# Feed-forward, context MLP and routing as one pipeline, and attention transposes one slot later

## The reference

```python
x = x + _L0_xattn_ref(_layernorm(x), ctx, ctx, mask0, bias, ...)   # attention, 16 heads of 16
x = x + _L0_ffn_ref(_layernorm(x), W_r, W_k, W_v, mu_r, mu_k)
x = x + _L1_xattn_ref(_layernorm(x), ctx, ctx)                     # gelu(x ctx^T) ctx
x = x + _L1_ffn_ref(_layernorm(x), w_router, w1, w2, w3)           # 8 experts, best 2
x = x + _L2_xattn_ref(_layernorm(x), ctx, ctx, W, b, mask2)        # attention, causal
x = x + _L2_ffn_ref(_layernorm(x), gate_w, shared..., r_...)       # shared + best 1 of 8
x = x + _L3_xattn_ref(_layernorm(x), ctx, ctx, Wq, Wk, Wv, Wo)     # attention, score 0 masked
x = x + _L3_ffn_ref(_layernorm(x), weight_int8, weight_scale, bias)
# inside _L0_ffn_ref, with x_prev the tokens shifted by one
r = sigmoid((mu_r * x + (1 - mu_r) * x_prev) @ W_r.T)
k = (mu_k * x + (1 - mu_k) * x_prev) @ W_k.T
out = r * (square(relu(k)) @ W_v.T)
```

## Time and profile before

| | us |
|---|---|
| median of 3 runs | 1191.1 (1186.71 to 1192.58) |
| the profiled execution, its own time | 1189.59 |
| span of its trace | 1187.9 |
| TensorE busy | 915.3 (77%) |
| VectorE busy | 567.6 (48%) |
| ScalarE busy | 424.1 (36%) |
| GpSimd busy | 404.0 (34%) |

### The profile page before, as it was taken

One profiled execution on the slowest core, in us unless ns is written; L12 is line 12 of the kernel. 1 busy time (PEld: TensorE's weight loads), 2 busy tenths in 40 slices (PEclk: granted clock), 3 DMA queues, 4 the chain that ended last, 5 costly groups with the idle time before them and its releaser, 6 DMA issues. The chain is left out here.

```text
span 1187.9 us, 18637 instructions
## 1 busy us (share of the span) xinstructions
PE 915.3 (77%) x5578; PEld 605.2 (51%) x5579; DVE 567.6 (48%) x1207; ACT 424.1 (36%) x820; POOL 404.0 (34%) x741
## 2 busy tenths in 40 slices
PE   6688757867229999963777867997999978877773
PEld 5455536643216777742444523664666655545541
DVE  4778845644431222225899713221121225777764
ACT  4355532312003333312666522221222213555644
POOL 5656634422470000016776411110000022666550
PEclk9899978968559999985899887998999996887885
DMA  5690001000121111124710030001111110000002
GB/s 169 241 327 1 1 4 45 0 10 0 49 102 49 62 62 62 62 68 159 293 32 19 1 107 22 23 26 58 36 44 44 40 46 14 15 14 14 1 1 71
DMA packets 60183, 71.25 MB, mean 60 GB/s; under 512 B 8172, under 2 KB 51924, under 8 KB 60116
## 3 DMA queue, kind: packets, MB, share of 16 engines
q1 hardware_dynamic: 55507, 57.81, 14.6%
q0 software_dynamic: 4608, 12.59, 3.2%
HBM read 45.73 MB, written 24.64 MB: 59 GB/s over the span
## 5 line engine op out<-in xcount | busy, mean ns | idle before, releaser
L1566 PE MATMUL PS<-WE,tmp 128*128 x496 | 185.8, 518 | 0.0
L1219 DVE TENSOR_TENSOR tmp<-PS,tmp 128x352 f32<-128x352 f32 (+1 forms) x78 | 47.4, 608 | 261.6 <-ACT tmp L858 261.6
L543 POOL TENSOR_TENSOR tmp<-tmp,small 128x616 f32<-128x616 f32 x96 | 116.7, 1216 | 102.1 <-DVE small L995 101.5
L1566 PEld LDWEIGHTS PS<-WE,tmp 128*128 128x128 f32 x496 | 91.5, 194 | 60.4 <-issue 36.1
L858 ACT ACTIVATE tmp<-PS 128x352 f32<-128x352 f32 (+1 forms) x78 | 41.4, 531 | 218.8 <-PE PS L1566 218.8
L771 ACT ACTIVATE tmp<-PS 128x768 f32<-128x768 f32 x96 | 77.9, 811 | 115.5 <-PE PS L1390 114.9
L1388 PE MATMUL PS<-ident,tmp 128*128 128x128 f32 x384 | 69.2, 309 | 45.1 <-POOL rsx L530 26.1
L1586 PE MATMUL PS<-WE,tmp 128*128 (+1 forms) x418 | 101.0, 380 | 2.1 <-DVE tmp L1231 2.1
L1301 PE MATMUL PS<-ident,XN 128*128 128x128 f32 x240 | 48.4, 337 | 68.2 <-ACT XN L707 54.0
L508 POOL DMA_INDIRECT WE<-ys,slot_u x32 | 32.5, 1015 | 182.4 <-DMA ys<-tmp 172.7
L644 POOL DMA_INDIRECT xs<-tmp,slot_u x48 | 46.6, 971 | 121.7 <-DVE tmp L1206 112.0
(11 more groups left out here) (210 smaller groups left out, 1620.8 us busy)
## 6 DMA issues: line engine op xcount, KB each, us to landing
tmp<-xs SPq DMA_DIRECT2D x62, 128.0 KB, 2.0
ys<-tmp SPq DMA_DIRECT2D x62, 128.0 KB, 1.7
xs<-WE SPq DMA_DIRECT2D x4, 1536.0 KB, 9.5
WE<-in_L_w SPq DMA_DIRECT2D x16, 352.0 KB, 6.9
WE<-in_L_rgT SPq DMA_DIRECT2D x8, 512.0 KB, 10.0
WE<-in_L_ruT SPq DMA_DIRECT2D x8, 512.0 KB, 10.2
WE<-in_L_rdT SPq DMA_DIRECT2D x8, 512.0 KB, 10.3
X<-in_x SPq DMA_DIRECT2D x8, 256.0 KB, 6.8
```

The costliest lines, as they stand in the source:

```text
L543: pool.tensor_tensor(sc, sc, spread(mx[:, q], SK), ALU.add).then_inc(shifted, 1)
L1219: dve.tensor_tensor(HH[:, q, 0:F], PS[:, 2 * q + 1, 0:F], SL[:, q, 0:F], ALU.mult).then_inc(hh_ready, 1)
L1566: last = pe.matmul(PS[:, 2 * q + k, 0:F], XS[:, q, c], w, start=c == 0, stop=c == G - 1)
```

## The change

1. f0, m1 and r1 with its scatter become one stage, f, of 12 slots (`F_SLOTS`). In slot s the engines do: keys and gates of batch s; values, sum, layernorm and transposes of the feed-forward of batch s-1; the MLP of batch s-2; the transposes, logits and best two experts (`two_experts`) of batch s-3; ranks, slots (`two_slots`) and four indirect DMAs of batch s-4.
2. So that a token's slot can be known before all tokens are routed, each expert has a region of 2176 rows in `xs1_regions` (8 regions and one tile: 137 tiles, all zeroed, 12 DMAs of up to 1.5 MB instead of 4). `expert_tables` afterwards works out which tiles are used, and SyncE reads each tile's first row from SBUF (`value_load`). The number of tiles in e1 is still 39.
3. The shifted tokens are multiplied by ScalarE instead of GpSimd (`previous`). The sigmoid is 0.5 * (1 + tanh(x / 2)), which leaves one activation table for the stage; compiled, the stage has one table load less than f0, m1 and r1. Normalising moves from VectorE to ScalarE.
4. `W_k`, `W_v`, the router's weights and the context are loaded during a0; only `W_r` and a2's output weights are loaded after it.
5. `value_blocks` for a2 run at the end of f, in eight PSUM banks without waiting for one another.
6. In all three attentions the transposes of unit s-3 follow the scores of unit s, the values are those of s-4, and on VectorE bias and maximum come ahead of the sums. The slots of the output projection, the residual and what follows are one later; those of the gathers and of the way in are two earlier.

The diff, cut to its core:

```diff
-        def out_proj_slot(b):
-            return UNITS * b + 7
+            return UNITS * b + 8
...
         def gather_slot(b, t, k, K):
-            return UNITS * b - 11 + t * 2 + k * (2 // K)
+            return UNITS * b - 13 + t * 2 + k * (2 // K)
...
         def in_transpose_slot(b):
-            return UNITS * b - 4
+            return UNITS * b - 6
...
+            xs1, xs2 = BUFS["e1"][0], BUFS["e2"][0]
+            for s in range(F_SLOTS):
+                if 0 <= s - 4 < B:
+                    scatter_rows(s - 4, 0)
+                if 0 <= s - 1 < B:
+                    deviations_and_shifts(F_NORM["ffn", s - 1], s - 1)
+                if 0 <= s - 2 < B:
+                    deviations_and_shifts(F_NORM["mlp", s - 2], s - 2)
+                if 0 <= s - 4 < B:
+                    scatter_rows(s - 4, 1)
...
+                    if 3 <= s < NU + 3:
+                        u = s - 3
+                        act.wait_ge(pt_psum, u0 + u + 1)
+                        after(act, ot_ready, (u0 + u) // 2 - 1 if u >= 4 else 0)
+                        act.activation(PT[:, u % 4], PT_PSUM, ACT.Copy).then_inc(pt_ready, 1)
...
+            for s in range(F_SLOTS):
+                if s < B:
+                    mixes(s)
+                if 0 <= s - 1 < B:
+                    add_ffn(s - 1)
+                    row_stats(F_NORM["ffn", s - 1], s - 1)
+                if 0 <= s - 4 < B:
+                    two_slots(s - 4)
+                if 0 <= s - 2 < B:
+                    add_mlp(s - 2)
+                    row_stats(F_NORM["mlp", s - 2], s - 2)
+                if 0 <= s - 3 < B:
+                    two_experts(s - 3)
+            expert_tables()
+            end_stage(dve, "f")
...
                     if 0 <= s < NU:
                         scores(s)
-                    if s == 3:
+                    if 3 <= s < NU + 3:
+                        transposes(s - 3)
+                    if s == 4:
                         pe.wait_ge(blocks_ready, 4 * (layer + 1))
-                    if 3 <= s < NU + 3:
-                        values(s - 3)
+                    if 4 <= s < NU + 4:
+                        values(s - 4)
...
-                    if 2 <= s < NU + 2:
-                        transposes(s - 2)
...
+            for i, banks in enumerate(FREE_BANKS):
+                if i == 3:
+                    pe.wait_ge(rank_taken, B)
+                value_blocks(1, i, banks)
+            end_stage(pe, "f")
```

More of the change, by code:

```diff
@@ L718, in attention @@
                 u0, q0 = NU * layer, 0 if stage == "a0" else B
[L719 removed]
+                order = ORDER[stage]
                 def queries(b):
@@ L1120, in running_sums, with mixes @@
                 return ping
-            def route(stage, first):
-                to = dict(r1="e1", r2="e2")[stage]
-                K, n_slots = TOPK[to], SLOTS[to]
+            def mixes(b):
+                dve.wait_ge(prev_ready, b + 1)
+                for dst, prev, k, used, ready in ((xkT, tB, 3, k_psum, k_mixed), (xrT, tA, 2, r_psum, r_mixed)):
+                    after(dve, used, b)
+                    for g in range(G):
+                        last = dve.scalar_tensor_tensor(out=dst[:, g], in0=XT[:, b, g, 1:S + 1], scalar=vecs[:, k, g:g + 1],
+                                                        in1=prev[:, g], op0=ALU.mult, op1=ALU.add)
+                    last.then_inc(ready, 1)
@@ new lines, in two_experts @@
+            def two_experts(b):
+                tiles = slice(b * T, (b + 1) * T)
+                dve.wait_ge(logits_psum, b + 1)
+                dve.tensor_copy(LG[:, tiles], PS[:, 4, 0:T * E].rearrange("p (t e) -> p t e", t=T)).then_inc(logits_copied, 1)
+                dve.drain()
+                first_of(LG[:, tiles], 0, tiles)
+                dve.scalar_tensor_tensor(out=count[:, 1, tiles], in0=hot[:, 0, tiles], scalar=NEG, in1=LG[:, tiles],
+                                         op0=ALU.mult, op1=ALU.add)
+                dve.drain()
+                first_of(count[:, 1, tiles], 1, tiles)
+                dve.tensor_tensor(taken[:, tiles], hot[:, 0, tiles], hot[:, 1, tiles], ALU.add).then_inc(pair_taken, 1)
@@ L1252, in _ @@
             dve.drain()
-            for i in range(B // 2):
-                value_blocks(1, i)
             experts("e1")
@@ new lines, in ffn_values, with mlp_hidden @@
+            def ffn_values(b):
+                pe.wait_ge(ksq_ready, b + 1)
+                after(pe, r_used, b)
+                two_tiles(6, ksq, W[:, 2]).then_inc(v_sum, 1)
+            def mlp_hidden(b):
+                pe.wait_ge(xt_ready, F_NORM["ffn", b] + 1)
+                after(pe, g_ready, b)
+                for c in range(G):
+                    last = pe.matmul(PS[0:SK, 2, 0:S], ctxT[:, c, b * SK:(b + 1) * SK], XT[:, b, c, 1:S + 1],
+                                     start=c == 0, stop=c == G - 1)
+                last.then_inc(g_psum, 1)
@@ new lines, in mlp_out, with logits @@
+            def mlp_out(b):
+                pe.wait_ge(g_ready, b + 1)
+                after(pe, c_taken, b)
+                for t in range(T):
+                    last = pe.matmul(PS[:, 3, t * D:(t + 1) * D], gel[:, t * P:(t + 1) * P], V[:, b], start=True, stop=True)
+                last.then_inc(c_psum, 1)
+            def logits(b):
+                pe.wait_ge(xt_ready, F_NORM["mlp", b] + 1)
+                after(pe, logits_copied, b)
+                for t in range(T):
+                    for c in range(G):
+                        last = pe.matmul(PS[:, 4, t * E:(t + 1) * E], XT[:, b, c, 1 + t * P:1 + (t + 1) * P], WR[:, c],
+                                         start=c == 0, stop=c == G - 1)
+                last.then_inc(logits_psum, 1)
@@ new lines, in _ @@
+            pe.wait_ge(w_loaded, 16 * 7)
+            pe.wait_ge(ctx_loaded, 16 * 2)
+            pe.wait_ge(tri_ready, 1)
+            for s in range(F_SLOTS):
+                if 0 <= s - 1 < B:
+                    ffn_values(s - 1)
+                if 0 <= s - 3 < B:
+                    transpose_rows(F_NORM["mlp", s - 3], ND[(s - 3) % 3])
+                if 0 <= s - 2 < B:
+                    mlp_hidden(s - 2)
+                if 0 <= s - 4 < B:
+                    ranks(s - 4)
+                if s < B:
+                    ffn_keys(s)
+                if 0 <= s - 2 < B:
+                    mlp_out(s - 2)
+                if 0 <= s - 3 < B:
+                    logits(s - 3)
+                if s < B:
+                    ffn_gates(s)
+                if 0 <= s - 1 < B:
+                    transpose_rows(F_NORM["ffn", s - 1])
@@ L1594, in experts @@
                 end_stage(pe, stage)
-            pe.wait_ge(w_loaded, 16 * 7)
-            route("r1", 0)
-            for i in range(B // 2):
-                value_blocks(1, i)
             pe.wait_ge(blocks_ready, 8)
```

547 lines of the change are left out of this document (289 added, 258 removed).

## The result

The changed kernel takes 1237.37 us (median of 4, 1230.33 to 1239.78) against 1191.32 us: the ratio is 1.038, with a 95% interval of 1.033 to 1.044. The prediction was 1136 us, with a range of 1110 to 1168, so the sign was wrong.

A forecast was written before the change was run, and what follows sets the result against it. No engine was taken as full from a0's end to e1's start; VectorE was taken as fullest in the attentions. 1189.6 - 32.6 - 9 - 2 - 11 = 1135, 1136 us with run-to-median difference; range 1110 to 1168.

The forecast's parts named there:

- part 2: a0: the wait of 1.48 us at the residual goes, period 13.0 us a batch; -9 us, range -10 to 0.
- parts 3 and 4: a2: nothing steady, -2 us, range -6 to +4; a3: ScalarE's copy no longer waits, -11 us, range -19 to +3.
- The attentions keep their periods: Rival, chance 0.15: in the attentions the same wait may only change its place; starts and tails alone left, 1167 us.
- part 4: a3: rsx transposes follow the next scores, ScalarE's copy stops waiting, 17.7 to 18.0 us a batch, start +6.8; -11 us.
- the term of +3.2: a2's start: first scores may come behind batch 1's transposes, 3.2 us after the first bias of the kernel before.
- the ramp's waits: a2's ramp: the bias waits, 6.9 us in all, were to go in part.
- Part 1: Stage f: full slots of 13.5 us, TensorE fullest at 12.7; e1 starts at 322.7, not 355.3; -32.6 us, range -40 to -8.
- the loop rival: Rival, chance 0.20: f's slot is one serial loop with handovers costing as in f0; 16.5 us a slot, +25, 1160 us.
- the clock rival: Rival, chance 0.04: TensorE's clock stays low in f; all slots at 1.2 GHz give +75, 1210 us.
- the rival had it at 1 us a tile: Rival, chance 0.03: SyncE's register loads do not hide in e1; 39 tiles give +39, 1175 us.
- The lead of 8.8 us: e1: SyncE reads the row address and fetches two tiles, 8.8 us, ahead, so e1 was left at zero.

The follow-up runs named there:

- f_only: The changed kernel with all three attentions written as before (part 6 undone), the stage f kept: 1161.58 us, ratio 0.977.
- The best version: Stage f, register load hoisted, two value blocks in f's last slots, a3 with later transposes, VectorE's old order and earlier blocks, a0 and a2 as before: 1136.43 us.

## Why the prediction was wrong

**The step that failed** is in part 2, and parts 3 and 4 lean on it: "what is late next is VectorE itself: 12.03 busy and 1.0 of drains, 13.0" (drains are the short gaps between VectorE's instructions: 14.50 less 12.03 less the wait of 1.48). The wait at the residual did go from the steady part, as the sentence ahead of it says. But the wait only changed its place, to the bias, and grew: the period of a batch is 17.15 us and not 13.0. What is late next was found by adding up busy time, and not by asking what the sums had been covering. In the old order the sums stood ahead of the bias in every slot and need nothing of this slot's scores. With them behind the bias, VectorE has little to do until the scores are there, and what TensorE does ahead of the scores (projection, queries, row transposes) becomes VectorE's wait; the reciprocals then come late, and TensorE's transposes and GpSimd's deviations with them. Putting back the sums alone (1166.1), putting back VectorE's whole order (1155.7) and changing only that order (1316.8 from 1161.6) show it from three sides. Its size in the sum: +26.0 in place of -9 in a0, +12.3 in place of -2 in a2, +38.6 in place of -11 in a3.

A reading helped it along. "VectorE is the fullest engine in all three" is not so in a0: the earlier trace rows has TensorE busy for 12.31 us of 14.50 and VectorE for 12.03. Where two engines are both nearly full and wait for each other in every slot, little room is left for a longer loop between them.

**The rivals.** "The attentions keep their periods" was near in kind (the same wait may only change its place), but had no price for a place that is worse. The range ended at the periods of before, although a reordering on both sides of a loop can lengthen it. The earlier trace rows shows TensorE waiting 3.21 us for rsx, and a reader could have seen there that rsx, transposes and scores are one loop, and that putting anything ahead of the sums feeds it.

**With VectorE's order put back, the forecast of part 4 holds** in its mechanism: the waits that it named go by the rest of part 6, and VectorE's new order had kept them. In a3 (us in all, times):

| | before | changed | changed, VectorE's order as before |
|---|---|---|---|
| TensorE's transposes for rsx | 22.5, 12 | 23.2, 16 | 2.5, 4 |
| the mask for ScalarE's scaled copy | 26.1, 16 | 45.4, 15 | 11.5, 9 |

a3 with q3 takes 205.4 and 205.5 us against 215.0, -9.6 where -11 was said. The start cost 7.5 us in the changed kernel (33.2 us from the stage's start to the first mask, against 25.7), where 6.8 was said. With the old order on VectorE the period in steady state is 18.7 us (masks at 1020.6 and 1076.6, three batches) against a forecast of 17.7 to 18.0. a0 gained between nothing and 2.6 us (136.0 and 133.2 against 135.8) in place of 9: the wait for the projection at the residual, 15.8 us in the run, stays when the residual is at the head, so the later transposes alone never took it away. a2 is 6 us longer, of which 5.2 lie in its start (27.5 us to the first bias, against 22.3 in f_only): the term of +3.2 was right in kind and too small, and the ramp's waits didn't go.

**Part 1, f.** -33.6 against -32.6 is partly luck. Slots 4 to 7 were faster than 13.5: from gates to gates (L1435 at 240.63, 250.63, 266.62, 277.86 and 289.49) they take 10.0, 16.0, 11.2 and 11.6 us. The first is TensorE's work with no wait, 10.0 where 12.7 was said; of that, the weight loads of logits and ranks are 1.9 (246.11 to 247.14 and 249.81 to 250.63) and not 3.6. Busy time of the first two slots, and the wait in the second:

```profile
240.63:250.63 10.00, 10.00 (x61) 8.66 (x60) 8.42 (x34) 6.79 (x14) 1.72 (x6) 1.00 0.00 0
250.63:266.62 15.99, 12.96 (x60) 10.82 (x60) 8.62 (x34) 6.94 (x14) 8.39 (x16) 0.79 0.12 43
...
255.63 1.11 PE L1413 MATMUL PS<-ident,XN 128*128 128x128 f32 x4 [3.03 <-ACT XN L724]
```

The slot of 16.0 is not the loop rival's 16.5. It has the wait for the normalised rows that the rival named, but with the clock kept such a slot takes 13.2 us; the rest is the clock, which fell after the wait. The same slot in the run with VectorE's order put back, after the same wait (3.02 us), kept the clock:

```profile
221.43:234.62 13.19, 10.17 (x61) 8.58 (x60) 8.42 (x34) 6.95 (x14) 7.70 (x16) 1.00 0.12 42
```

So the clock rival, priced as all slots at 1.2 GHz, did not come, but 2.8 us of one slot are the clock's. What the slots gained was lost in the tail: TensorE's waits there are 4.65, 1.66, 3.35 and 3.25 us, and after the first of them the granted clock is 0.50 until e1 starts (304.47 to 348.00). The best version fills part of these waits. The zeroing, the tables and the scatters were hidden, as forecast.

**e1** was left at zero on the ground that the fetch goes two tiles ahead; the rival had it at 1 us a tile with a chance of 0.03. It was 0.2 us a tile. The lead of 8.8 us was wrong already for the kernel before. The fetch's own wait allows it two tiles ahead, but it stands on SyncE behind the store of an older tile, and so it went out 2.4 us before it was needed (442.87 for 445.24). With the register load in that piece 2.0 us were left, and TensorE waited. The 1 us for a load was taken from no row.

## What to carry to other kernels

When operations change places on an engine, ask of each what it waits for in this slot, and let work that needs nothing new stand first: it covers the waits of the rest. Busy time plus the gaps between instructions is the next bound only if no loop between the engines got longer; write the loop out, scores to scores, before and after. An address that is read into a register belongs ahead of the last wait before the transfer, not behind it. How far ahead a transfer goes is read from its issue in the trace, not from its lag in the program.

## What the hardware showed

TensorE's granted clock was lower where TensorE waited more, and that makes waits dearer. a0 has the same 1120 matmuls in every version; they are busy for 105.2 us at 0.94, 120.0 at 0.84 and 136.5 at 0.76, as the stage goes from 134.7 to 161.8 and 186.7 us. So of the 26 us that a0 lost, up to 13.7 are the same matmuls run at a lower clock (106.3 before, 120.0 now); which of them lie on the chain the runs don't tell. The prediction had priced no wait with the clock in it.

The same wait does not always cost the same. In f's second full slot TensorE waited 3.0 us for the normalised rows in all thirteen traces with the stage f. In two (the changed kernel and the one with part 6 undone) the clock of the slot was then 0.79 and it took 16.0 us; in three it was 0.88 and 14.7 us, and in the other eight the slot took 13.2 us, with a clock of 1.00 in those measured. The stage f as a whole took 145.5 and 145.6 us in the first two, and 142.7 to 143.1 in the ten others with the same f, so the three made up for it elsewhere. What decides it no run shows. The waits of 1.06, 1.46 and 1.74 us in the next slots were not followed by a lower clock, the one of 4.65 us was. Eight transposes in a slot did not hold the clock down: three of the four full slots of the changed kernel had 1.00.
